# Storing a decoder's filler rows during attention, and routing the last group in halves

## What is computed

```python
x = x + attn(layernorm(x))                       # causal window of 128 keys + first 16 keys, 16 heads of 16
x = x + xattn(layernorm(x), ctx, ctx, mask)      # 64 context rows per sequence, 16 heads
x = x + ffn(layernorm(x))                        # below
```

```python
def ffn(x):                                      # x: S = 8 sequences, B = 512 positions
    y = layernorm(x + mha(x, ...), g1, be1)      # 4 heads of 64, attends over the 8 sequences of a position
    xf = y.reshape(S * B, D)
    idx = argmax(xf @ Wg.T, axis=-1)             # one of 8 experts for each row
    out = zeros_like(xf)
    for e in range(8):
        out = out + (idx == e) * (relu(xf @ W1[e] + b1[e]) @ W2[e] + b2[e])   # 256 -> 1024 -> 256
    return layernorm(y + out, g2, be2)
```

## Time and profile before

| | |
|---|---|
| median of 3 runs | 1238.98 us (1237.64 to 1239.57) |
| the profiled execution | 1236.71 us |
| its span, first to last instruction | 1235.0 us |
| TensorE busy | 1157.7 us (94%) |
| VectorE, ScalarE, GpSimd busy | 761.1, 529.3, 507.5 us |
| mean granted clock of TensorE | 0.99 |
| moved by DMA | 103.75 MB, mean 84 GB/s |
| attention, mixing, experts | to 685, to 936, to 1235 us of the span |

### The profile page before, as it was taken

One profiled execution on the slowest core, in us unless ns is written; L12 is line 12 of the kernel. 1 busy time (PEld: TensorE's weight loads), 2 busy tenths in 40 slices (PEclk: granted clock), 3 DMA queues, 4 the chain that ended last, 5 costly groups with the idle time before them and its releaser, 6 DMA issues. The chain is left out here.

```text
span 1235.0 us, 27567 instructions
## 1 busy us (share of the span) xinstructions
PE 1157.7 (94%) x8842; PEld 785.8 (64%) x8851; DVE 761.1 (62%) x2126; ACT 529.3 (43%) x1123; POOL 507.5 (41%) x718
## 2 busy tenths in 40 slices
PE   8999999999999999999898799999999999999995
PEld 3546465464554645546454466666667999999995
DVE  4555667766767577675636466667673656565653
ACT  5445454545545454544442255444523333333330
POOL 3334325244252442523421122443353556655664
PEclk9999999999999999999999999999999999999998
DMA  7233324043231441323202233435214111111110
GB/s 221 73 97 105 106 75 127 25 117 108 71 109 46 111 113 52 89 68 81 78 15 81 89 96 119 144 109 174 88 38 133 49 44 50 51 55 51 52 44 7
DMA packets 110012, 103.75 MB, mean 84 GB/s; under 512 B 29688, under 2 KB 103294, under 8 KB 109824
## 3 DMA queue, kind: packets, MB, share of 16 engines
q1 hardware_dynamic: 103632, 89.49, 25.4%
q0 software_dynamic: 5280, 12.66, 3.0%
q10 hardware_dynamic: 1040, 0.83, 0.2%
HBM read 49.41 MB, written 16.75 MB: 54 GB/s over the span
## 5 line engine op out<-in xcount | busy, mean ns | idle before, releaser
L960 ACT ACTIVATE probs<-ps_b 128x512 f32<-128x512 f32 (+2 forms) x352 | 174.5, 538 | 91.7 <-PE ps_b L1427 36.5
L583 POOL TENSOR_SCALAR_AFFINE_SELECT probs<-probs 128x512 f32<-128x512 f32 x128 | 81.6, 637 | 267.0 <-ACT probs L960 263.6
L2843 PE MATMUL ps_c<-keep_w,e_hT 128*128 x624 | 141.0, 379 | 0.0
L2843 PEld LDWEIGHTS ps_c<-keep_w,e_hT 128*128 128x128 f32 x624 | 115.7, 190 | 14.1
L702 DVE CUSTOM_DVE_ANT_0 ps_a<-ps_a,mask_qk 128x256 f32<-128x256 f32 x224 | 88.9, 450 | 18.9 <-PE ps_a L1251 18.8
L696 DVE TENSOR_REDUCE top<-ps_a 128x2 f32<-128x512 f32 (+1 forms) x112 | 74.1, 683 | 29.4 <-PE ps_a L1251 28.5
L1251 PE MATMUL ps_a<-k_rows,q_rows 96*128 96x256 bf16 (+1 forms) x512 | 84.5, 260 | 4.6 <-DVE top L702 2.7
L2804 ACT ACTIVATE e_yT<-ps_d 128x256 f32<-128x256 f32 x39 | 14.9, 383 | 171.3 <-PE ps_d L2822 171.3
L1806 ACT ACTIVATE e_w_now<-keep_w 128x1024 f32 x78 | 78.0, 1049 | 22.0 <-issue 11.8
L2832 PE MATMUL ps_a<-e_yT,e_w_now 128*128 128x128 f32 x640 | 75.9, 277 | 0.0
L1282 PE MATMUL ps_b<-q_rows,k_rows 98*128 98x256 bf16 (+1 forms) x512 | 75.3, 259 | 0.2
(11 more groups left out here) (249 smaller groups left out, 2453.0 us busy)
## 6 DMA issues: line engine op xcount, KB each, us to landing
q_rows<-parts SPq DMA_DIRECT2D x96, 128.0 KB, 2.4
k_rows<-parts SPq DMA_DIRECT2D x96, 128.0 KB, 2.4
q_rows<-q_parts SPq DMA_DIRECT2D x96, 128.0 KB, 2.4
keep_w<-in_e_w SPq DMA_DIRECT2D x16, 512.0 KB, 4.4
keep_w<-in_e_w SPq DMA_DIRECT2D x8, 1024.0 KB, 8.1
e_row<-sorted_rows SPq DMA_DIRECT2D x38, 130.0 KB, 2.1
x_in<-in_x SPq DMA_DIRECT2D x8, 512.0 KB, 4.6
x_res<-in_x SPq DMA_DIRECT2D x8, 512.0 KB, 5.1
```

The source lines that it names most:

```text
L583: nc.gpsimd.affine_select(own, own, [[0, TILES], [1, P]], ALU.is_ge, keep_zero, base=0, channel_multiplier=-1).then_inc(probs_cut.sem, 1)
L960: nc.scalar.activation(probs[:, user % 2, lo:lo + width], ps_exp[:, f % 2, 0:width], ACT.Exp).then_inc(exp_done.sem, 1)
L2843: mm = nc.tensor.matmul(ps_out[:, s, 0:D], hT[:, s, f, :], w2[:, bass.ds(e * KF * D + f * D, D)], start=(f == 0), stop=(f == KF - 1))
```

## The change

- The filler tile moves to attention, where GpSimd sets it at the start. SyncE stores it in attention: the whole region of expert n after the mask load of sequence n, 4224 rows by one DMA of 33 rows for each partition, and the ten spare blocks behind the last one. The block waits for these stores at its end.
- The ten spare stores of group 0, the eight stores of `fill_ends` and their table of rows go, and the waits for them. `tile_rows`, a constant for the tables, is loaded at the start of mixing and no longer in attention; VectorE waits for it with the weights before the tables.
- The last routing runs in halves: `choose` and `slots` on tiles 0 and 1, then on tiles 2 and 3; TensorE ranks the first half before the logits of the second; GpSimd sends the first half's rows when their places are known. The sharing order gets the names for it.
- Row block 1 is loaded by SyncE behind block 0. ScalarE copies only step 0's weights before the barrier, and step 1's in the expert stage behind its copies of features 0 and 1.
- Filling matmuls: 8 more at the end of attention, 14 for 10 at the start of mixing, 2 for 3 in the tail, 36 for 50 at its end.

The diff, cut to its core; the operations of `choose` and `slots` are the same ones on the slice `own`, with counts `part + 1`:

```diff
+        filler = sb("filler", [P, ROW])
...
+                def fill_rows(dst, count):
+                    sp.dma_start(dst, filler[:, :].unsqueeze(1).broadcast_to([P, count, ROW])).then_inc(rows_filled.sem, 16)
...
                     if first:
                         for dst, src in later_loads:
                             sp.dma_start(dst, src).then_inc(later_loaded.sem, 16)
+                        sp.wait_ge(consts_set.sem, 12)
+                    fill_rows(t["sorted"][0:E * REGION, :].rearrange("(e p k) w -> e p k w", e=E, p=P)[n], REGION // P)
+                    if last:
+                        fill_rows(t["sorted"][E * REGION:, :].rearrange("(p k) w -> p k w", p=P), SPARE_TILES)
...
                 sp.wait_ge(later_loaded.sem, 16 * len(later_loads))
+                sp.wait_ge(rows_filled.sem, 16 * (E + 1))
...
+                nc.gpsimd.memset(filler[:, 0:D], 0.0).then_inc(consts_set.sem, 1)
+                nc.gpsimd.memset(filler[:, D:ROW], NO_TOKEN).then_inc(consts_set.sem, 1)
                 low_parts(-1, range(4))
...
                 closing(B - 1, B)
+                keep_warm(ps_max[:, 0, :], 8)
...
+HALVES_FILLS = ["out0", "out1", "yT0", "logits0", "yT1", "ranks0", "logits1", "ranks1"]
...
                 sp.dma_start(keep["b1"][:, :], t["e_b1"]).then_inc(weights_loaded.sem, 16)
+                sp.dma_start(tile_rows[:, :], t["c_tile_rows"]).then_inc(weights_loaded.sem, 16)
...
-                sp.wait_ge(consts_set.sem, CONSTS_SET)
-                for i in range(SPARE_TILES):
-                    sp.dma_start(t["sorted"][E * REGION + i * P:E * REGION + (i + 1) * P, :],
-                                 filler[:, :]).then_inc(filler_sent.sem, 16)
...
-                fill_ends(sp, range(0, E, 2))
                 sp.wait_ge(weights_loaded.sem, WEIGHT_LOADS)
                 sp.wait_ge(tables.sem, TABLE_STEPS)
                 all_rows_written(sp)
-                ahead.load_row(t, sp, keep, 0, 0)
+                for j in range(2):
+                    ahead.load_row(t, sp, keep, j, j)
...
-                nc.gpsimd.memset(filler[:, :], 0.0).then_inc(consts_set.sem, 1)
-                pool.wait_ge(consts_set.sem, CONSTS_SET - 2)
-                nc.gpsimd.memset(filler[:, D:D + 1], NO_TOKEN).then_inc(consts_set.sem, 1)
+                pool.wait_ge(consts_set.sem, CONSTS_SET - 1)
...
-                send_rows(NGROUPS)
+                for part in range(2):
+                    send_rows(NGROUPS, (2 * part, 2 * part + 1), part)
...
-                    choose(n)
-                    slots(n)
+                    for k, own in enumerate((first_half, second_half)):
+                        choose(n, own, k, f"logits{k}")
+                        slots(n, own, k, f"ranks{k}")
...
-                    dve.wait_ge(next_row_kept.sem, NGROUPS + 1)
-                    nc.vector.tensor_copy(filler_row[:, :], next_row[:, 0, :]).then_inc(tables.sem, 1)
+                    dve.wait_ge(next_row_kept.sem, next_row_kept.count(NGROUPS, 2))
+                    dve.wait_ge(weights_loaded.sem, WEIGHT_LOADS)
...
-                fill_ends(act, range(1, E, 2))
                 act.wait_ge(tables.sem, TABLE_STEPS)
                 act.wait_ge(weights_loaded.sem, WEIGHT_LOADS)
-                for j in range(2):
-                    ahead.take_weights(nc, act, keep, j, j)
-                all_rows_written(act)
-                ahead.load_row(t, act, keep, 1, 1)
+                ahead.take_weights(nc, act, keep, 0, 0)
...
-                keep_warm(10)
+                keep_warm(14)
...
-                logits(NGROUPS, (0, 1))
+                logits(NGROUPS, (0, 1), "logits0")
                 keep_warm(5)
                 y_features(NGROUPS, (1,))
-                keep_warm(3)
-                logits(NGROUPS, (2, 3))
+                keep_warm(2)
+                ranks(NGROUPS, slice(0, 2), 0, "ranks0")
+                logits(NGROUPS, (2, 3), "logits1")
                 keep_warm(5)
-                ranks(NGROUPS)
-                keep_warm(50)
+                ranks(NGROUPS, slice(2, TILES), 1, "ranks1")
+                keep_warm(36)
...
                 for j in range(2):
                     features(j, j)
+                ahead.take_weights(nc, act, keep, 1, 1)
                 rounds(act, step)
```

More of the change, by code:

```diff
@@ L2205, in choose, with slots @@
+                    nc.vector.tensor_reduce(first[:, own], order[:, own, :], AX.X, ALU.max).then_inc(first_ready.sem, 1)
+                    dve.wait_ge(first_ready.sem, first_ready.count(n, part + 1))
+                    nc.vector.tensor_tensor(chosen[:, own, :], order[:, own, :], first[:, own].unsqueeze(2).broadcast_to(wide),
                                             ALU.is_equal).then_inc(chosen_ready.sem, 1)
-                def slots(n):
-                    wide = [P, TILES, E]
-                    bank = work_take(dve, n, "ranks")
+                def slots(n, own, part, name):
+                    wide = [P, own.stop - own.start, E]
+                    bank = work_take(dve, n, name)
@@ L2251, in iteration @@
                     if route:
-                        choose(n)
+                        choose(n, whole, 0, "logits")
                     take_output(n, 2)
                     if route:
-                        slots(n)
+                        slots(n, whole, 0, "ranks")
                     take_output(n, 3)
@@ L2500, in y_features, with logits @@
                         mm.then_inc(work_full.sem, 1)
-                def logits(n, tiles=range(TILES)):
-                    ps = work_claim(pe, n, "logits")
+                def logits(n, tiles=range(TILES), name="logits"):
+                    ps = work_claim(pe, n, name)
                     for c in tiles:
@@ L2508, in logits, with ranks @@
                             mm = nc.tensor.matmul(ps[:, c * E:(c + 1) * E], yT_half(c // 2)[:, k, (c % 2) * P:(c % 2 + 1) * P], w_g[:, k, :],
-                                                  start=(c == 0 and k == 0), stop=(k == KD - 1), skip_group_check=True)
-                    if TILES - 1 in tiles:
-                        mm.then_inc(work_full.sem, 1)
-                def ranks(n):
-                    ps = work_claim(pe, n, "ranks")
-                    pe.wait_ge(chosen_ready.sem, chosen_ready.count(n, 1))
-                    nc.tensor.matmul(ps[:, 0:TILES * E], before[:, :], chosen[:, :, :].rearrange("p c e -> p (c e)"),
+                                                  start=(c == tiles[0] and k == 0), stop=(k == KD - 1), skip_group_check=True)
+                    mm.then_inc(work_full.sem, 1)
+                def ranks(n, own=slice(0, TILES), part=0, name="ranks"):
+                    ps = work_claim(pe, n, name)
+                    pe.wait_ge(chosen_ready.sem, chosen_ready.count(n, part + 1))
+                    nc.tensor.matmul(ps[:, own.start * E:own.stop * E], before[:, :], chosen[:, own, :].rearrange("p c e -> p (c e)"),
                                      start=True, stop=False, skip_group_check=True)
-                    for c in range(TILES - 1):
-                        later = TILES - 1 - c
-                        mm = nc.tensor.matmul(ps[:, (c + 1) * E:TILES * E].rearrange("p (c e) -> p c e", e=E), ones16[:, :],
+                    for c in range(own.start, own.stop - 1):
+                        later = own.stop - 1 - c
+                        mm = nc.tensor.matmul(ps[:, (c + 1) * E:own.stop * E].rearrange("p (c e) -> p c e", e=E), ones16[:, :],
                                               chosen[:, c, :].unsqueeze(1).broadcast_to([P, later, E]), start=False,
                                               stop=True, skip_group_check=True)
-                    for c in range(TILES):
+                    for c in range(own.start, own.stop):
                         mm = nc.tensor.matmul(ps[:, TILES * E:(TILES + 1) * E], ones16[:, :], chosen[:, c, :], start=False,
```

71 lines of the change are left out of this document (29 added, 42 removed).

## The result

| | before | after |
|---|---|---|
| runs timed beside the first result | 4, median 1238.52 us | 4, median 1231.09 us (1229.53 to 1232.96) |
| ratio, 95% interval | | 0.995 (0.9937 to 0.9962) |
| profiled execution, its span | 1236.71, 1235.0 us | 1232.96, 1231.3 us |

The change is faster by 0.5%. Two later repeats of the same kernel, against 25 and 27 more runs of before, gave ratios of 0.9953 and 0.9954: 5.7 us. So the question is where some 1.7 us beyond the forecast come from. The two profiled executions cannot tell: their spans differ by only 3.7.

The account below looks back on a forecast made before the run. TensorE, busy in nearly every slice, was taken as the bound, with gains only at the two passages between stages: 0 + 0.5 + 3.5 = 4.0 us off the median 1238.98 gives 1235.0 us, range 1232.5 to 1240.

Parts of the forecast that it names:

- The fills at 0: Attention: eight fills of 15.5 us each at 283 GB/s hide in gaps of the DMA queue and cost 0.
- 17.5 + 2.1: Sequence 0, the tightest place: 17.5 us free for a fill, after 2.1 for the shift rows' own landing.
- the slow fill: Rival in attention: a fill outlasts its gap; at 24 us a fill the kernel takes 1241.5 us; chance 0.12.
- the drain: Rival at the passage to the experts: GpSimd's drain, at 6.4 us, holds the barrier; 1237.7 us; chance 0.14.
- halves that don't hide: Rival at the last routing: the slots come 2 us later, 2.0 of gain left, 1237 us; chance 0.08.
- The passage to the experts at 3.5: Barrier opens at about 932.5, the first expert product starts at about 934.2 instead of 937.80: 3.5 us gained.
- The passage to mixing at 0.5: Eight more filling matmuls shrink TensorE's idle from 2.28 to about 0.5 us and keep the clock: 0.5 us gained.
- I let the clock fall as today: 0: At the experts' start 1.9 us of idle remain, so the half clock was taken to stay as before: 0.
- The rival that the clock stays up there: At the expert stage the shorter idle keeps the clock up: gain 5.3 us, 1233.7 us; chance 0.20.
- The base: The median of three runs of the kernel before, 1238.98 us, from which the forecast gain was taken.
- theory K: Follow-up theory, not in the prediction: TensorE idles of 1.5 us or more bring half-clock stretches, 1.1 to 1.7 us each.

Follow-up runs that it names:

- fills_added: The kernel before with the nine fills added in attention, its own eighteen filler stores kept: 1237.09 us against 1237.14, ratio 0.9995.
- warm_more: The changed kernel with 42 for 36 filling matmuls before the experts, nine more in mixing group 0, seven in the last sequence: 1228.43 us, ratio 0.9941.

## Why the prediction was right or wrong

- **The fills at 0**: right. They go at 246 to 269 GB/s where I took 283, so that the one in sequence 0 was down 2 us later than I had it (19.7 us after its issue, where I had 15.5 and a landing of 2.1; 17.7 to 20.6 in the nine profiles with fills). None held TensorE, though the longest went beyond the 17.5 + 2.1 that I had taken for the limit; so that limit was too narrow, and when the shift rows land no trace shows. The rivals of the slow fill, of the drain (2.68 again) and of halves that don't hide (the first instruction on the finished counts comes 0.3 sooner, 15.17 us after the last output product's start instead of 15.47) are out.
- **The passage to the experts at 3.5**: right, 3.72 in the pair of profiles that I worked with (29.20 to 25.48); the product started at 933.83, where I had 934.2. Over all profiles it is 4.0 (means 29.4 of six with the old passage, 25.4 of six with the new one). The path was the one forecast: ScalarE's conversions open the barrier (done at 931.9, where I had 932.4), and row block 1 is what TensorE waits for last ahead of the product (its transposes start at 933.35; I had the load landed at 933.7). That the parts are all needed is shown for two: with whole routing GpSimd holds the barrier, with the end stores SyncE does, and each alone brings about half. A third was never taken away by itself, the step from two converted weight slices to one. Two instructions take 2.00 us after and four took 3.9 before, so ScalarE would have been done some 1.9 later with both slices, an estimate.
- **The passage to mixing at 0.5**: this is the step that failed. I wrote "With the clock kept the transposes, which are on the path, end up to 0.9 earlier", and priced the clock only at the place where it falls. There it gives 0.1, less the 0.34 by which the eight matmuls hold the barrier back, so the term by itself is slightly negative. What the kept clock is worth lies further on: the stretch at 690 comes with one in group 0. For the 0.5 of my sum the runs with these matmuls alone measured 1.5 and 1.9 us (ratios 0.9988 and 0.9985); and 1.9 is lost when they are taken out of the changed kernel, there with overlapping intervals. I had not written the stretches at 711 and 800 into the sum at all, though a row of mine has a PEclk of 0.86 in group 0.
- **"I let the clock fall as today: 0"** at the experts: half wrong. It stays up in some executions (two of four profiles), worth 1.4 to 1.6 each. The rival that the clock stays up there, with a chance of 0.20 and a gain of 5.3, is the nearest in number to the measured 5.7. That is in part luck: it had the place half right, and had nothing of the stretches in mixing, which make up the larger share (1.5 to 1.9 above, against half of 1.4 to 1.6).
- **The sum again**: passage to the experts 3.7 to 4.0, barrier of mixing -0.3, fills 0, and a mean clock that rises from 0.990 to 0.992 (0.9899 and 0.9902 to 0.9922 and 0.9921 in the two jobs with repeats). 0.0021 x 2 x 1236 is 5.2 us less at half clock, or 1.5 stretches of 3.4, at 1.2 to 1.7 each 1.8 to 2.6. Together 5.2 to 6.3, against 5.7 measured. The mean clock also counts the 8 to 12 us at half clock behind the last matmul, which cost nothing; they are about as long before as after (means 10.6 and 10.9 in three profiles each), so the difference hardly depends on them.
- **The base**: 1238.98 was the median of three runs. Before then gave 1237.14, 1235.61 and 1237.24 over 73 runs in three jobs, so part of the number missed is not the change's. As a ratio the forecast was 0.9968: outside the interval of the first result and on the slow edge of both repeats' intervals.

What I overlooked: TensorE idles 6.4 to 6.7 us between 20 and 98 us of the span in the six profiles made from the kernel before, fills_added among them, and 6.1 to 6.2 in the eight made from the changed one. The difference is a wait at 73.8 for ScalarE's read of scores, which the eight don't have. So up to 0.35 us of the gain lie in sequence 0 and come neither from the fills nor from the clock; the cause stays open.

What stays open too: which executions get a stretch and which don't. After, TensorE waits for key rows in sequence 1, and the clock falls behind it:

```profile
141.50 0.60 PE L1258 MATMUL ps_a<-mask_qk,ident 128*128 128x512 bf16 x1 [1.58 <-DMA k_rows<-parts]
```

Before waited 1.68 us at the same place, and its clock stayed up. This wait is 0.7 to 1.7 us long from one execution to the next, with and without fills, and spreads the times by itself. A wait without a sure stretch is also the one of 1.61 us in the last sequence, which every profile but warm_more has: six of thirteen show a stretch between 654 and 657 behind it. And theory K is too strong as I wrote it: the stretches at 673, 775 and 800 to 908 have no idle time of 1.5 us ahead of them. At 800 TensorE comes from sixteen logits products of eight columns each. That the second stretch follows from the first, at 690 and 712, is a regularity of fourteen profiles; no run separated the two.

## What to carry to other kernels

A short idle of TensorE can cost nearly as much again as its own length: here one of 1.6 to 2.5 us may bring 3.4 us at half clock, mostly 1.2 to 1.7 us of time. So list the stretches of PEclk below 1 and the idle ahead of each first, fill these with matmuls that end just before the wait does (here the profiles lost their stretches; that the time falls by the last such additions isn't clear of noise), and take several profiled executions before a difference of two microseconds is given to a cause. At a barrier several engines can be due within a few us of each other; making one of them earlier wins only the distance to the next, here about half.

## What the runs showed of the hardware

- The kernel before, profiled three times, had its stretches at half clock at different places, four or five of them ahead of the last matmul. The Trainium skill (TensorE: Matmul & The Clock Gate, Part 1: The HAM clock gate) says of the start of a kernel that the number of slow matmuls varies from run to run; here the trace shows it in the middle of a kernel.
- GpSimd's drain at the end of the mixing block is 2681 ns to the nanosecond in all fourteen profiles, with whole or halved sends and with or without end stores beside them. It starts 0.3 us after the last send's landing (932.92 and 933.19 before, 928.02 and 928.28 after). At this place it is a fixed price; at the kernel's end it is 6427 ns in all fourteen.
- Stores of 1040 B rows, 33 from one source row, reach 246 to 269 GB/s with the other traffic and don't slow TensorE: 15.66 us busy in 16 against 15.58, and a median of 1237.09 against 1237.14 when they are added to the kernel before.
